# A vision tower on one core: each engine's instruction order of a step rewritten, waits by token tile and PSUM bank, one evicting engine per bank

## The reference

```
x   = patches(8x8) @ conv_w + conv_b                      # 256 tokens of width 128
for i in range(2):
    q, k, v = split(LN(x, ln1[i]) @ qkv_w[i])             # 8 heads of 64
    q = softmax(q, features) * 64**-0.5 ; k = softmax(k, tokens)
    x = x + (q @ (k^T v)) @ out_w[i] + out_b[i]           # linear attention
    x = x + gelu(LN(x, ln2[i]) @ ff1_w[i] + ff1_b[i]) @ ff2_w[i] + ff2_b[i]
h   = LN(x, lnf) @ head_w + head_b                        # width 192
h   = h + attn(layernorm(h))     # 12 heads of 16, phi = elu + 1, z = 1/(q . sum k + eps)
h   = h + ffn(layernorm(h))      # 192 -> 768 -> 192, tanh gelu, weights scaled by mixed masks
```

## Time and profile before

| | |
|---|---|
| median of 3 runs | 133.97 us (133.22 to 134.89) |
| profiled execution | 134.81 us, span 133.0 us, mean granted clock 0.987 |
| PE matmul busy | 116.9 us (88%), 934 instructions |
| DVE busy | 78.0 us (59%) |
| ACT busy | 66.7 us (50%) |
| POOL busy | 54.3 us (41%) |
| input | 11.09 MB read, nearly all before 36 us |

### The profile page before, as it was taken

One profiled execution on the slowest core, in us unless ns is written; L12 is line 12 of the kernel. 1 busy time (PEld: TensorE's weight loads), 2 busy tenths in 40 slices (PEclk: granted clock), 3 DMA queues, 4 the chain that ended last, 5 costly groups with the idle time before them and its releaser, 6 DMA issues.

```text
span 133.0 us, 2464 instructions
## 1 busy us (share of the span) xinstructions
PE 116.9 (88%) x934; PEld 104.2 (78%) x934; DVE 78.0 (59%) x225; ACT 66.7 (50%) x149; POOL 54.3 (41%) x65
## 2 busy tenths in 40 slices
PE   6979899998899898998989899389974999999991
PEld 6979787986778777787877787279963979999991
DVE  1000567996599455994569944764867799265001
ACT  4001245904769946799568996038233150931520
POOL 0000260182756737576246855575294350022000
PEclk9999999999999999999999999968999999999999
DMA  4999999707910000000000000000000000000101
GB/s 112 367 409 402 411 407 413 267 4 285 245 24 0 2 5 0 0 0 5 0 0 0 5 2 0 0 0 2 0 5 0 0 0 0 0 5 0 59 0 59
DMA packets 3947, 11.63 MB, mean 87 GB/s; under 512 B 448, under 2 KB 1568, under 8 KB 3936
## 3 DMA queue, kind: packets, MB, share of 16 engines
q1 hardware_dynamic: 3936, 11.48, 24.0%
HBM read 11.09 MB, written 0.39 MB: 86 GB/s over the span
## 4 chain that ended last, share of the span: by engine, by line
PE 46%; DVE 28%; DMA 7%; POOL 6%; issue 5%; SPq 3%; ACT 2%; DVEq 0%; POOLq 0%; ACTq 0%
PE bank L331 17%; DMA patches_sb<-in_patches 7%; PE bank L596 6%; PE bank L489 4%; PE bank L465 4%; DVE q L764 4%; DVE nqmax L759 4%; DVE nkmax L752 3%; POOL qn L1161 3%; DVE xn L686 3%; PE bank L355 2%; PE bank L457 2%; DVE qsum L771 2%; PE bank L566 2%; SPq L281 2%
## 5 line engine op out<-in xcount | busy, mean ns | idle before, releaser
L1138 POOL TENSOR_TENSOR rstd<-mv,minus_half 128x2 f32<-128x2 f32 x14 | 9.9, 709 | 40.1 <-DVE mv L681 40.1
L1161 POOL TENSOR_TENSOR qn<-q,rqsum 128x512 f32<-128x512 f32 x8 | 8.2, 1044 | 9.0 <-DVE rqsum L776 9.0
L1015 ACT ACTIVATE kexp<-bank,nkmax 128x256 f32<-128x256 f32 x16 | 7.4, 471 | 7.3 <-DVE nkmax L752 7.0
L465 PE MATMUL bank<-cw,qT 128*128 128x128 f32 x64 | 10.0, 289 | 0.0
L465 PEld LDWEIGHTS bank<-cw,qT 128*128 128x128 f32 x64 | 8.2, 190 | 1.6 <-issue 0.8
L355 PE MATMUL bank<-embed_sb 128*128 128x128 f32 x64 | 8.4, 290 | 0.8 <-DMA embed_sb<-in_embed 0.8
L355 PEld LDWEIGHTS bank<-embed_sb 128*128 128x128 f32 x64 | 8.1, 202 | 1.2 <-DMA embed_sb<-in_embed 1.2
L355 PE MATMUL bank<-embed_sb,patches_sb 128*128 128x128 f32 x64 | 8.2, 280 | 0.6 <-DMA patches_sb<-in_patches 0.6
L1010 ACT ACTIVATE qkvw_hi<-qkvw 128x512 fp32r<-128x512 f32 x3 | 1.9, 631 | 13.4 <-DMA qkvw<-in_qkv_w 13.4
L686 DVE TENSOR_SCALAR xn<-x,mv,rstd 128x128 f32<-128x128 f32 x20 | 6.0, 342 | 4.4 <-POOL rstd L1138 4.4
L1156 POOL TENSOR_TENSOR xb<-x,rows_sb 128x256 f32<-128x256 f32 x8 | 6.4, 800 | 5.3 <-DVE xn L686 5.3
(11 more groups left out here) (137 smaller groups left out, 330.9 us busy)
## 6 DMA issues: line engine op xcount, KB each, us to landing
patches_sb<-in_patches SPq DMA_DIRECT2D x4, 512.0 KB, 10.8
embed_sb<-in_embed SPq DMA_DIRECT2D x2, 768.0 KB, 7.0
restw<-in_rest_w SPq DMA_DIRECT2D x2, 768.0 KB, 14.5
embed_sb<-in_embed SPq DMA_DIRECT2D x2, 384.0 KB, 8.4
qkvw<-in_qkv_w SPq DMA_DIRECT2D x3, 256.0 KB, 9.6
embed_sb<-in_qkv_w SPq DMA_DIRECT2D x1, 768.0 KB, 5.3
embed_sb<-in_embed SPq DMA_DIRECT2D x1, 576.0 KB, 4.3
projw_raw<-in_proj_w SPq DMA_DIRECT2D x1, 576.0 KB, 15.0
```

The lines of the kernel that those rows point to most:

```text
L465: mm = nc.tensor.matmul(VB[0][:, t * D:(t + 1) * D], qT[i][:, t, c * P:(c + 1) * P], cw[i][:, c, :], start=(c == 0), stop=(c == PAIRS - 1))
L1015: nc.scalar.activation(kexp[i][:, c, :], KB[c // 2][:, (c % 2) * TOKENS:(c % 2 + 1) * TOKENS], ACT.Exp, bias=nkmax[i][:, c:c + 1], accum_o ...
L1138: nc.gpsimd.tensor_tensor(rstd[i][:], mv[i][:, :, 1], minus_half[:], ALU.pow).then_inc(rstd_ready[i], 1)
L1161: nc.gpsimd.tensor_tensor(qn[i][:, t, :].rearrange("p (h d) -> p h d", h=HEADS), q[i][:, t, :].rearrange("p (h d) -> p h d", h=HEADS), rqs ...
```

## The change

Nothing that is computed changes and no transfer changes size; the two halves of some evictions and waits are redrawn.

- **Order on PE.** In a step: q tile 0 high; k chunks 0 and 2 high and weight-low; then chunks 2, 3 (bank 1) finished, then 0, 1 (bank 0); q; v high of both tiles; turn of LN2; the rest of v; `turn_k` (tile 1 first); `ff1`; `context`; **`ff2` ahead of `turn_q` 0**; `context_out` split into two halves around `turn_q` 0; `turn_q` 1; `attend` 0; turn of LN1; all of `attend` 1. `ff2` finishes tile 0 ahead of tile 1.
- **One evicting engine per bank.** LN1: DVE takes tile 0 (`yT_hi` and `yT`) from bank 6, ACT tile 1 from bank 7, and DVE makes `yT_lo` of both. LN2: ACT makes `yT_hi` and `yT`, POOL `yT_lo` as before. `ktok`: DVE both tiles. `vtok`: ACT tile 0, DVE tile 1. `qT`: ACT both tiles. `cw`: ACT chunks 0, 2, 3, DVE chunk 1. `attend` writes tile `t` to `VB[t]`.
- **Waits by tile.** `xn_ready`, `x_ready`, `x_mid`, `x_new`, `att_done`, `ff2_done`, `turned` count tiles instead of pairs; the moments of tile 0 start while tile 1 is still being added.
- **Tables.** `load_table(ACT.Exp)` stands right behind `gelu` in steps 1 and 2, and explicit loads stand ahead of the third attention's exponentials and the last gelu.
- **Side work.** DVE's `mix_alpha` goes to the start, `mix_masks` and `mix_sum` to either side of LN1's apply in the first step; ACT's weight high parts go to the end of the steps; POOL's `mix_fc` both to step 2, four of six `mix_proj` to step 3, qkv1's parts 1 and 2 ahead of `normalise_q` in step 1.
- **Tail.** `head`, `qk3`, v3, `context_out3`, `attend3`, `fc3` and `proj3` are re-ordered in the same manner: v3 in parts around `head(1)`, `context_out3` ahead of `turn_q3`, both `attend3` behind the LN3 turn, `fc3` of the second image with its high parts first, `proj3(1)` finishing tile 0 ahead of tile 1.

The core of the diff (PE's step, DVE's step, ACT's step, POOL's step):

```
# PE, step s
-                qkv_q(l, i, "high")
-                qkv_k(l, i)
-                qkv_q(l, i, "low")
-                qkv_v(l, i, 0)
+                pe.wait_ge(tile0_ready[i], 2 * l + 1)
+                q_part(l, i, 0, "high")
+                pe.wait_ge(tile1_ready[i], 2 * l + 1)
+                k_part(l, i, 0, "high")
+                k_part(l, i, 2, "high")
+                k_part(l, i, 2, "weight_low")
+                k_part(l, i, 0, "weight_low")
+                pe.wait_ge(yT_lo_ready[i], LOW[LN1(l)])
+                k_part(l, i, 2, "low")
+                k_chunk(l, i, 3).then_inc(k_done[i], 1)
+                k_part(l, i, 0, "low")
+                k_chunk(l, i, 1).then_inc(k_done[i], 1)
+                q_part(l, i, 1, "high")
+                q_part(l, i, 0, "weight_low")
+                q_part(l, i, 0, "low").then_inc(q_done[i], 1)
+                q_part(l, i, 1, "weight_low")
+                q_part(l, i, 1, "low").then_inc(q_done[i], 1)
+                if s:
+                    pe.wait_ge(x_mid[ip], TILES * (lp + 1))
+                v_part(l, i, 1, "high")
+                v_part(l, i, 0, "high")
                 if s:
                     turn_norm(ip, LN2(lp), SB_)
-                qkv_v(l, i, 1)
+                v_part(l, i, 0, "weight_low")
+                v_part(l, i, 0, "low").then_inc(v_done[i], 1)
+                v_part(l, i, 1, "weight_low")
+                v_part(l, i, 1, "low").then_inc(v_done[i], 1)
                 turn_k(l, i)
                 if s:
                     ff1(lp, ip)
                 context(l, i)
-                turn_q(l, i, 0)
                 if s:
                     ff2(lp, ip, FF2)
-                context_out(l, i)
+                context_out(l, i, 0)
+                turn_q(l, i, 0)
+                context_out(l, i, 1)
                 turn_q(l, i, 1)
-                attend(l, i, 0, 0, PAIRS)
-                attend(l, i, 1, 0, PAIRS // 2)
-                turn_norm(1 - i, LN1((s + 1) // 2), HALVES if s < STEPS - 1 else CB)
-                attend(l, i, 1, PAIRS // 2, PAIRS)
+                attend(l, i, 0)
+                if s < STEPS - 1:
+                    turn_norm1(1 - i, (s + 1) // 2, HALVES)
+                attend(l, i, 1)
...
# DVE, step s (new order)
+                k_max(l, i, 1)
                 k_max(l, i, 0)
                 if s:
                     norm_apply(ip, LN2(lp), x[ip], D)
-                k_max(l, i, 1)
                 q_max(l, i, 0)
-                if s:
-                    norm_out_hi(ip, LN2(lp), SB_, col("ln2_g", lp), col("ln2_b", lp))
+                q_max(l, i, 1)
                 q_shift(l, i, 0)
-                q_max(l, i, 1)
                 q_shift(l, i, 1)
+                k_to_sbuf(l, i, 1)
                 k_to_sbuf(l, i, 0)
+                v_to_sbuf(l, i, 1)
                 q_sum(l, i, 0)
+                k_inverse_sum(l, i)
                 q_inverse_sum(l, i, 0)
                 q_sum(l, i, 1)
-                k_inverse_sum(l, i)
+                context_blocks(l, i)
                 q_inverse_sum(l, i, 1)
+                if s:
+                    for t in range(TILES):
+                        add_ff(lp, ip, t, FF2)
+                        add_moments(ip, LN1(lp + 1), x[ip], t, D, x_new[ip], TILES * lp + t + 1)
+                    for t in range(TILES):
+                        close_moments(ip, LN1(lp + 1), t, D, t + 1)
+                else:
+                    for t in range(TILES):
+                        x_from_conv(1, t)
+                    norm_stats(1, LN1(0), x[1], D, x_ready[1], 1, 1)
+                    mix_masks()
+                context_scaled(l, i, 1)
+                norm_apply(1 - i, LN1((s + 1) // 2), x[1 - i], D)
+                if s == 0:
+                    mix_sum()
+                add_attention(l, i, 0)
+                if s < STEPS - 1:
+                    norm1_tile0(1 - i, (s + 1) // 2, SB_)
+                    norm1_low(1 - i, (s + 1) // 2)
+                add_moments(i, LN2(l), x[i], 0, D, x_mid[i], TILES * l + 1)
+                add_attention(l, i, 1)
+                close_moments(i, LN2(l), 0, D, 1)
+                add_moments(i, LN2(l), x[i], 1, D, x_mid[i], TILES * l + 2)
+                close_moments(i, LN2(l), 1, D, 3)
...
# ACT, step s (new order)
                 k_exp(l, i)
                 if s:
-                    norm_out(ip, LN2(lp), SB_, col("ln2_g", lp), col("ln2_b", lp))
-                q_exp(l, i, 0)
+                    norm2_high(ip, lp, SB_)
+                    norm2_full(ip, lp, SB_)
+                v_to_sbuf(l, i, 0)
                 for t in range(TILES):
-                    v_to_sbuf(l, i, t)
-                k_to_sbuf(l, i, 1)
-                q_exp(l, i, 1)
+                    q_exp(l, i, t)
                 if s:
                     gelu(lp, ip)
+                    if s < STEPS - 1:
+                        load_table(ACT.Exp)
-                context_scaled(l, i)
+                context_scaled(l, i, 0)
+                context_scaled(l, i, 2)
+                q_to_sbuf(l, i, 0)
+                context_scaled(l, i, 3)
                 q_to_sbuf(l, i, 1)
-                ln = (s + 1) // 2
                 if s < STEPS - 1:
-                    norm_out_halves(1 - i, LN1(ln), HALVES, col("ln1_g", ln), col("ln1_b", ln))
+                    norm1_tile1(1 - i, (s + 1) // 2, CB)
...
# new evictions of LN1 (DVE, then ACT)
+            def norm1_tile0(i, l, bankof):
+                g, b = col("ln1_g", l), col("ln1_b", l)
+                dve.wait_ge(turned[i], TURNED[LN1(l)] - 1)
+                nc.vector.tensor_scalar(yT_hi[i][:, 0:P], bankof[:, 0:P], g, b, ALU.mult, ALU.add).then_inc(tile0_ready[i], 1)
+                nc.vector.tensor_scalar(yT[i][:, 0:P], bankof[:, 0:P], g, b, ALU.mult, ALU.add).then_inc(tile0_ready[i], 1)
+            def norm1_tile1(i, l, bankof):
+                g, b = col("ln1_g", l), col("ln1_b", l)
+                at = slice(P, 2 * P)
+                act.wait_ge(turned[i], TURNED[LN1(l)])
+                nc.scalar.activation(yT_hi[i][:, at], bankof[:, at], ACT.Identity, bias=b, scale=g).then_inc(tile1_ready[i], 1)
+                nc.scalar.activation(yT[i][:, at], bankof[:, at], ACT.Identity, bias=b, scale=g).then_inc(tile1_ready[i], 1)
...
# POOL, step s (new order, s > 0)
+                    rsqrt(ip, LN2(lp))
+                    after_norm(ip, LN2(lp))
+                    if s == 1:
+                        qkv1_low_part(0)
+                    else:
+                        add_bias(ip, "ff2_b", lp, x_mid[ip], TILES * (lp + 1))
+                    if s == 2:
+                        weight_low_part("ff1_1", 1, ff1w_all(1), ff1w_parts[1][0][:], ff1w_parts[1][1][:])
+                    if s == 3:
+                        aqkv_low_part(0)
+                    norm2_low(ip, lp)
+                    if s == 1:
+                        add_bias(ip, "ff2_b", lp, x_mid[ip], TILES * (lp + 1))
+                        qkv1_low_part(1)
+                        qkv1_low_part(2)
+                    if s == 2:
+                        for c in range(ECH):
+                            mix_fc(c)
+                    if s == 3:
+                        mix_proj(0, 4)
                 for t in range(TILES):
                     normalise_q(l, i, t)
```

827 lines of the change are left out of this document (418 added, 409 removed).

## The result

The changed kernel takes **127.98 us** (median; 127.14 to 130.83) against 134.29 (133.22 to 134.89) for the kernel before, measured beside it. The ratio is 0.952, with a 95% interval of 0.942 to 0.961. The forecast was 126.8, in a range of 124.4 to 131.5. Its sign and range held; it was 1.2 us too low. The ratio leaves out the longest run, 130.83, as a slow one; the median has it.

What follows compares the result with a forecast made beforehand. No engine was full, PE nearest, losing time to waits in a chain through PE, DVE and POOL. Terms of 1.1 + 4.9 + 1.1 + 0.9 + 0.8 = 8.8, less 1.6, gave 126.8 us on the median's scale, range 124.4 to 131.5.

Steps and rivals of the forecast that it cites:

- first step, to the start of step 1: First step: turn one conv chunk earlier, k maxima sooner, attends waiting about 1 us for mix_masks; minus 1.1 us (0 to 1.5).
- step 3, to the head: Last of three like steps, counted at the same saving as the others: minus 1.65 us.
- head to qk3: From step 3 to qk3: shorter LN2 wait, possibly 2.4 GHz kept (1.5 more); minus 1.1 us in all (0.3 to 2.4).
- attention 3, first image: Stage from 92.56 us: evictions covered by reordering, minus 1.1, phi3_exp plus 0.2; net minus 0.9 (plus 0.3 to minus 1.3).
- the rest: From 104.93 us on: waits near the k sums minus 0.5, one output leaving early minus 0.3 (in all 0.2 to 1.2).
- kept back: 1.6 us held off the sum for waits a hand schedule misses: about 0.3 per step and 0.4 for the tail.
- The middle step: One step worked part by part: vtok at 7.43 us sets context, step 14.6 us against 16.28, minus 1.65.
- the ten pieces on DVE: DVE's run ahead of context: two k_max, norm_apply, two q_max, two q_shift, two ktok copies, one vtok; 5.92 us.
- other moved work keeps its waits: POOL's and SP's moved work: same transfers issued, qkv1's starting with conv_done, about 0.5 us earlier.
- rival 1: ACT becomes the loop: 10.2 us path with 0.1 slack, each step 1 us late; 129.5 us; chance 0.18.
- rival 2: The waits only move: DVE's ktok/vtok run keeps context back, steps give 0.4; 132.0 us, within 2%; chance 0.10.
- rival 3: Slower through POOL: qn behind about 5.5 us of other POOL work per step, stretched 1.7 times; 137.2 us; chance 0.05.

Runs made afterwards that it cites:

- early load: Layer 1's qkv weights in an SBUF tile of their own, transfer issued ahead of rest_w 1, in the changed kernel: 127.38 us, ratio 0.943.
- filler: Unread matmuls in three PE pauses, added to the changed kernel with the early load: 126.94 us (four, four, eight), 126.41 us (two, two, three).
- the statistics first: Changed kernel with the early load; in attention 3 DVE takes the other image's norm statistics ahead of q times k sum, kv before denominator: 126.99 us, ratio 0.940.

## Why the prediction was right, and where it was off

Its terms against the two traces of the changed kernel, in us against the profiled execution of before (predicted; first trace; second trace):

```
first step, to the start of step 1   -1.1    -1.54   -2.08
step 1                               -1.65   +1.29   +0.40
step 2                               -1.65   -1.39   -1.40
step 3, to the head                  -1.65   +0.14   +0.14
head to qk3                          -1.1    -2.70   -1.58
attention 3, first image             -0.9    +0.49   -0.73
the rest                             -0.8    -0.29   -0.25
kept back                            +1.6
sum                                  -7.2    -4.0    -5.5
```

The medians are 6.3 us apart. Both traces are of long executions: over all eight runs of the changed kernel the median is 128.5, and these took 130.83 and 129.3.

That the total came out near is partly luck. By ideal queues the forecast was 8.8; the 1.6 kept back were meant for small waits in each step, and they and the better first step also paid for a landing and a third step that the working had wrong.

**The middle step** was right, mechanism and size. The wait at its start went; the ten pieces on DVE set the context: vtok at 7.55 us (predicted 7.43), the context at 7.65 (7.47), and 7.24 from there on (7.15). Together 14.9 instead of 14.6, which is the 0.3 per step that was kept back for what a hand schedule misses. The wait stands where it was named, 0.27 long. (The list of matmuls that bounds the gain adds up to 13.45 us, not 13.6; nothing else hangs on it.)

**What failed is the sentence that POOL's and SP's "other moved work keeps its waits".** It counted the start of layer 1's transfer, but put no time on its landing. The weights' high part stands directly ahead of k's exponential, in both kernels. ACT came to it 1.5 to 2.1 us earlier than before, and the weights landed 7.2 to 8.1 us behind their issue, not 5.3. That made step 1 longer by 2.05 to 2.94 than predicted. The early load gave it back (14.80), and the same edit in the old order gave nothing. What made the landing later stays open.

**Step 3** was counted like a middle step, and saved nothing up to the head. Of a middle step's saving 0.64 is the wait at the next step's first product. Behind step 3 comes the head, for which PE waited only 0.30 in the old order, since half of `attend` covered the eviction. The new order has all of `attend` ahead of that turn: the turn and a wait of 0.75 stand uncovered.

**Head to qk3** was forecast at minus 1.1 as one figure for two cases: by its parts 0.8 to 0.9 if the clock falls as before, 1.5 more if it doesn't. It measured 1.58 with the fall and 2.70 without, so the waits gave more than their term (the one for LN2 went from 1.49 to 0.24) and the clock less (1.12). Some of it is step 3's loss given back: the head comes later, so the norm behind it is waited for less. Step 3 and this stretch together are minus 2.56 in the first trace, where the parts had minus 4.0 with the clock kept, and minus 1.44 in the second, where they had minus 2.5: about 1.1 to 1.4 short.

**Attention 3** was forecast at minus 0.9 and is minus 0.73 at the 2.4 GHz level (11.64). The forecast took the clock as a matter of the stage ahead alone. That stage did keep its clock in the first trace; but the level then fell at 97 us, behind the wait of 1.51, and took 1.22 back. In the second trace it fell in the stage ahead and took 1.12 there. With the pauses filled it fell in no run.

**The first step** was better than forecast, for two reasons. The stage itself (first q product to first q product) has 15.11 instead of 16.30, where it was to lose 1 us at `mix_masks`: at 0.74 that row no longer holds `cw` up. The price of 1.58 came from a row that ran beside POOL's. The remainder is the earlier start of the first q product, at 18.23 and 17.68 instead of 18.58. Counted from the first product with the second image's patches (14.68, 14.13 and 14.26), for which PE waits on their transfer, it is 3.55 us in both traces where it was 4.32: 0.77 is the order's, the turn being earlier and the first product needing only tile 0. What is left of the difference, 0.42 later and 0.13 earlier, is when the inputs landed.

**The rest** was mis-sized: 0.3 instead of 0.8. PE was already busy for 16.95 of 17.26 us in the earlier trace rows, and the output of tile 0, which is written early (126.07), cannot end the kernel sooner when tile 1's is written at 126.65. No run took this term apart.

**ACT as the loop** (rival 1) did not come about, but is near: 0.5 us more on it cost 0.2 to 0.3 a step. The tables were priced rightly at 1.28 each; the place of the Exp load, with hardly any slack by the forecast, mattered in step 3 alone. In the first trace a load starts as the last exp ends, gelu follows 0.01 us behind it, and no row of ACT shows a drain. The Trainium skill, ScalarE: Activation LUTs, section What ACT_TABLE_LOAD costs, has about 2.66 us a switch; the trace does not agree here.

**The waits only move** (rival 2) is true of one part alone: ff2 ahead of the turn of q costs 3.0 us in the trace and 4.0 by the medians in the old order, and taking it back costs as much in the new one (3.7 in the trace; 131.49 against 127.38, ratios of 0.974 and 0.943 to the kernel before). It works only when gelu's hid comes earlier too; which of the other parts (DVE's, ACT's, the banks) are needed for that was not taken apart. **POOL** (rival 3) did not stretch: `qn` has 2.04 for its two in step 2, from 59.87 to 61.91. PE turns tile 0 at 62.21, about 1.3 us behind the end of the first, and tile 1 at 63.38, 1.5 behind the end of the second.

## What to carry to other kernels

When an order of instructions changes, look again at every transfer whose landing used to be hidden, how far it may vary, and what is queued behind the instruction that waits for it. Give a repeated step's saving to the last one only after looking at what follows it. Compare stages between marks that both kernels have. When PE waits for an engine that has no gap of its own, the row that PE waits for is not the cause; add up that engine's run, and move work into a gap of it, not to its end. Parts of a rescheduling must be judged together: one alone can cost what it brings in company.

## What the runs showed of the hardware

**The clock follows pauses of PE, not their cause.** Behind a pause of 1.36 to 1.51 us, or two of 0.75 close together, the granted clock fell to the 1.2 GHz level for 3 to 4 us. It did so in 15 of 32 runs of the new order without filler, and not always behind the same pause: of the eight traces one has it at 44 us, three at 81 to 83, one at 97, three nowhere. The same pause of 1.50 at attention 3 stands in six of them and was followed by a fall in one. No trace has it twice, though one run without a trace (130.25 us, mean clock 0.973) had about twice the loss of clock. It cost 1.1 to 1.2 us in three traces and 1.4 in a fourth (head to qk3 of 7.85 us against 6.48, with the statistics first). A few matmuls without use in the pauses kept the 2.4 GHz level in all of 14 runs. Whether filling one pause alone would only hand the fall on to the next, no run tells.

**Two engines with two SBUF inputs each.** DVE's `weighted` row took 1.58 us beside POOL's `qn` and `xb`, and 0.74 when only a part of POOL's rstd lay beside it, while that rstd took 1.14 instead of 0.70. The Trainium skill, SBUF — State Buffer, section SBUF: two separate sides, says that DVE and GpSimd share a port pair that one instruction holds to its end when DVE reads two SBUF inputs; the rows agree. Before, `weighted` started at 27.28 while POOL's second `qn` ran to 28.22; 0.74 from there gives 28.96, and it ended at 28.86. Now rstd starts at 29.95 while `weighted` runs to 30.53; 0.70 from there gives 31.23, and it ended at 31.09. No run here measured it by itself.

**Landing times.** The same 768 KB, issued once the patch products were done and with 432 and 576 KB issued behind them, landed 5.3 and 5.2 us behind their issue in two traces of the old order, 8.1 and 7.2 in two of the new. Whether the order or chance makes the difference is open.
